# Attention's output product, sum and norm by token halves, and a later entry of the second half into the gated expert network

## The reference

```python
x = x + L2_xattn(layernorm(x), ctx, ctx, Wq, bq, Wk, bk, Wv, bv, Wo, bo)
x = x + L2_ffn(layernorm(x), router_w, w_gate, w_up, w_down)

def _pruned_attention(q, k, v):            # 16 heads of width 8, per batch
    scores = softmax(q @ k.T / sqrt(8))
    keep = int(S * 0.9)
    col_sum = scores.sum(axis=queries)
    mask = top_k(col_sum, keep)            # keys kept, per head
    return (scores * mask) @ v             # then @ Wo.T + bo

def _L2_ffn_ref(x, router_w, w_gate, w_up, w_down):   # 8 experts, top 2
    cw = normalised top-2 weights of softmax(x @ router_w.T)
    for e in experts:
        acc += cw[:, e] * ((silu(x @ wg[e]) * (x @ wu[e])) @ wd[e])
```

## Time and profile before

| what | value |
|---|---|
| median of 3 runs | 847.29 us (846.08 to 850.32) |
| profiled execution, its own time | 840.29 us |
| its span, first to last instruction | 838.6 us |
| mean granted TensorE clock | 0.920 of full |
| pruned attention's last steps, hand-over and step 0 of ffn2 | about 594 to 625 us of the span |
| plain attention's end | about 71 to 79 us of the span |

### The profile page before, as it was taken

How to read it: one execution, slowest core, us unless ns; L and a number is a source line. 1 busy time by engine, 2 the same in 40 slices (tenths; PEclk the granted TensorE clock), 3 DMA queues, 4 the chain that set the end, 5 groups by cost and what they waited for, 6 DMA issues and landing times. The chain is left out here.

```text
span 838.6 us, 14511 instructions
## 1 busy us (share of the span) xinstructions
PE 725.6 (87%) x4910; PEld 605.2 (72%) x4910; DVE 558.4 (67%) x1478; ACT 416.3 (50%) x1279; POOL 373.8 (45%) x375
## 2 busy tenths in 40 slices
PE   6884799998899999988579999699769999994755
PEld 3553699997899998876467887466558888883754
DVE  6897664355899998874746776668555565655535
ACT  3991344344455555552245776489334466651221
POOL 6753312202566643533214775664331588872001
PEclk9898799999999999997879999779779999996678
DMA  7000011110000000000004443000101322100000
GB/s 271 2 1 26 14 42 36 50 50 1 1 1 2 7 2 1 2 1 0 20 23 150 128 137 132 1 2 2 39 26 36 106 87 89 62 2 1 1 0 25
DMA packets 14276, 33.11 MB, mean 39 GB/s; under 512 B 1744, under 2 KB 5864, under 8 KB 13952
## 3 DMA queue, kind: packets, MB, share of 16 engines
q1 hardware_dynamic: 14208, 32.26, 11.6%
HBM read 31.63 MB, written 0.62 MB: 38 GB/s over the span
## 5 line engine op out<-in xcount | busy, mean ns | idle before, releaser
L1210 PE MATMUL banks<-input_hi,weights_in_lo 128*128 128x512 f32 x296 | 125.2, 423 | 17.8 <-PEq L1571 9.7
L1210 PE MATMUL banks<-input_lo,weights_in_hi 128*128 128x512 f32 x296 | 120.1, 406 | 0.0
L1210 PE MATMUL banks<-input_hi,weights_in_hi 128*128 128x512 f32 x296 | 119.7, 404 | 0.0
L1210 PEld LDWEIGHTS banks<-weights_out,hidden 128*128 128x128 f32 x864 | 100.5, 192 | 8.1 <-issue 5.1
L1210 PE MATMUL banks<-weights_out,hidden 128*128 128x128 f32 x864 | 101.6, 276 | 5.2 <-PEq L1524 4.5
L987 ACT ACTIVATE probabilities<-banks,neg_max 128x128 f32<-128x128 f32 x256 | 90.7, 430 | 13.2 <-DVE neg_max L1896 13.2
L1076 ACT ACTIVATE hidden<-banks,cols 128x512 f32<-128x512 f32 x80 | 54.1, 688 | 77.6 <-ACTq L1074 77.6
L697 POOL TENSOR_TENSOR rstd<-var_eps,neg_half 128x4 f32<-128x4 f32 x24 | 24.8, 1034 | 145.4 <-POOLq L696 130.3
L1210 PEld LDWEIGHTS banks<-input_hi,weights_in_lo 128*128 128x128 f32 x296 | 58.5, 198 | 31.9 <-issue 19.1
L807 POOL TENSOR_TENSOR hidden<-hidden,scratch 128x512 f32<-128x512 f32 x48 | 62.0, 1292 | 19.3 <-ACT hidden L1095 16.6
L1210 PEld LDWEIGHTS banks<-input_hi,weights_in_hi 128*128 128x128 f32 x296 | 58.2, 197 | 13.2
(11 more groups left out here) (272 smaller groups left out, 1754.4 us busy)
## 6 DMA issues: line engine op xcount, KB each, us to landing
scratch<-cw_rows SPq DMA_DIRECT2D x19, 512.0 KB, 4.0
weights_out<-w_in SPq DMA_DIRECT2D x17, 256.0 KB, 2.7
weights_in<-w_in SPq DMA_DIRECT2D x8, 512.0 KB, 3.6
weights_in<-w_in SPq DMA_DIRECT2D x9, 256.0 KB, 3.1
weights_in<-w_in SPq DMA_DIRECT2D x16, 128.0 KB, 2.2
weights_out<-w_in SPq DMA_DIRECT2D x16, 128.0 KB, 2.1
wq<-w1q_in SPq DMA_DIRECT2D x1, 1024.0 KB, 4.8
wo<-w1o_in SPq DMA_DIRECT2D x1, 1024.0 KB, 6.9
```

The lines of the kernel that those rows point to most:

```text
L1210: return pe.matmul(o, l, rh, start=start, stop=stop, **kw)
```

## The change

1. `attention_output` takes a half and a bank on TensorE and VectorE. In the plain attention both halves are still done at the end, in banks 4 and 5, but half 0 waits only for its own four blocks of `attT`.
2. In the pruned attention half 0's product is a stage of TensorE's list, `first_output`, in step 17, behind the last column sums, into bank 0. Its sum, statistics and norm are a stage of VectorE's list in step 19, behind the last `keep_values` and ahead of the last `scale_kept` (step 20).
3. After the attention TensorE turns half 0 of `xn` first and then makes half 1's product, into bank 7. VectorE runs `split_input(0)`, then half 1's sum, statistics and norm.
4. `second_half_at` is `(1, 0)` for every network: ffn2's second half is turned, taken and split at the head of step 1.

GpSimd's and SyncE's code is unchanged.

```diff
             def second_half_at(self):
-                return (0, 2) if self.FC == 4 and self.E > 1 else (1, 0)
+                return (1, 0)
...
+            def attention_output(prune, weight, half, at):            # TensorE
+                pe.wait_ge(out_copied[prune], (2 if prune else 4) * (half + 1))
+                for i in range(4):
+                    b = 4 * half + i
+                    m = mm(b4(at)[:, i, :], attT[:, b * P:(b + 1) * P], weight)
+                m.then_inc(y_attn_done, 1)
...
+                def first_output(it, n):
+                    pe.wait_ge(exps_done[prune], 8 * 15)
+                    attention_output(prune, w("wo2"), 0, 0)
...
-                                   (column_sums, range(UNITS), 2), (values_kept, last, 5)],
+                                   (column_sums, range(UNITS), 2), (first_output, (0,), 17),
+                                   (values_kept, last, 5)],
...
-            def attention_output(prune, weight):
-                pe.wait_ge(out_copied[prune], 4 if prune else 8)
-                for b in range(NB):
-                    m = mm(b4(4 + b // 4)[:, b % 4, :], attT[:, b * P:(b + 1) * P], weight)
-                    if b % 4 == 3:
-                        m.then_inc(y_attn_done, 1)
...
-                    if s == 0:
-                        transpose_half(0, source, f.output_bank(0))
-                    if s == 1 and f.FC == 2:
-                        transpose_half(1, source, f.output_bank(1))
+                    if s == 0 and not f.gated:
+                        transpose_half(0, source, f.entry_bank(0))
+                    if s == 1:
+                        transpose_half(1, source, f.entry_bank(1))
...
-                        if s == 0 and f.FC == 4 and fc == 2:
-                            transpose_half(1, source, f.output_bank(1))
...
-            attention_output(False, w("wo0"))
+            attention_output(False, w("wo0"), 0, 4)
+            attention_output(False, w("wo0"), 1, 5)
...
             narrow_attention(True)
-            attention_output(True, w("wo2"))
+            transpose_half(0, xn, ffn2.entry_bank(0))
+            attention_output(True, w("wo2"), 1, 7)
             mixed(ffn2, None, xn, w("r2"))
...
+            def attention_output(half, at):                           # VectorE
+                if half == 0:
+                    dve.wait_ge(x_bias_ready, 1)
+                    dve.sem_inc(x_bias_ready, -1)
+                dve.wait_ge(y_attn_done, 1)
+                dve.sem_inc(y_attn_done, -1)
+                part = x[:, 4 * half:4 * half + 4, :]
+                dve.tensor_tensor(part, part, b4(at), ALU.add).then_inc(st.sem, st.one())
+                norm_stats(half, x, 1e-5)
...
+                def first_output(it, n):
+                    attention_output(0, 0)
+                    norm_apply(0, x, xn, norm_tok_ready)
...
-                                    (keep_values, last, 4), (scale_kept, last, 5), (rank_first, last, 2),
+                                    (keep_values, last, 4), (first_output, (0,), 19), (scale_kept, last, 5),
+                                    (rank_first, last, 2),
...
-                            if (s, fc) == (0, 2):
+                            if (s, fc) == f.second_half_at():
                                 split_input(1)
...
             narrow_attention(True)
-            attention_output()
-            for half in range(2):
-                norm_apply(half, x, xn, norm_tok_ready)
             split_input(0)
+            attention_output(1, 7)
+            norm_apply(1, x, xn, norm_tok_ready)
             mixed(ffn2, [])
```

More of the change, by code:

```diff
@@ L1494, in hidden @@
                     for fc in range(f.FC):
-                        if source is not None and first and (n, fc) == (0, 2) == f.second_half_at():
-                            transpose_half(1, source, f.entry_bank(1))
                         if f.FC == 4 and begun and not f.gated:
@@ L1990, in narrow_attention @@
                                     (copy_both, range(UNITS), 2)], UNITS, 1, st.close)
-            def attention_output():
-                dve.wait_ge(x_bias_ready, 1)
-                dve.sem_inc(x_bias_ready, -1)
-                for half in range(2):
[L1997 to L2001, removed]
             def mlp_norm(half, *args):
@@ L2337, in _ @@
             narrow_attention(False)
-            attention_output()
+            attention_output(0, 4)
+            attention_output(1, 5)
             for half in range(2):
```

## The result

The changed kernel takes 835.83 us (median of 4 executions, 833.65 to 838.15) where the kernel before takes 848.68 (4 executions): ratio 0.9852, 95% interval 0.9809 to 0.9894. The profiled execution took 833.65 us, 6.6 less than that of before, close to the forecast of 834.3. The two numbers don't agree: 6.6 by the profiles, 12.9 by the medians. Later executions settle it in between. The 81 executions of before that were timed beside the experiments have a mean of 844.4 us (standard error 0.3), and 17 of the changed kernel one of 835.8 (0.6): 8.6 us.

What follows compares the result with a forecast made beforehand. One chain passing between engines from keep_values to the gated network bounds the hand-over. Step 1 earlier 5.77, plain attention 0.74, clock -0.5: 6.0 us saved, 847.29 to 841.3 us, range 837.5 to 845.5.

Steps and rivals of the forecast that it cites:

- the early passes before 598: TensorE ahead of the mask: half 0's eight product passes fit into 2.51 us of idle time, priced at nothing.
- a new pause before step 1: Gated network: four turned blocks, then TensorE idle 2.2 to 2.5 us before step 1, a sign of being right.
- signs of being wrong: TensorE waiting for half 1's product or norm, gates holding half 1's split, clock 0.50 over much of step 1, late GpSimd power.
- The plain attention: End of the plain attention: half 0's product need not wait for the last block's scaling, 0.74 us saved.
- The later entry: Half 1 turned at step 1's head: gives back 2.4 of 8.2 us, so step 1 begins 5.77 earlier.
- the rest shifts as a block: Behind step 1 of the gated network: all that follows is shifted by whatever step 1 is shifted.
- The clock, both ends: TensorE's clock: 0.85 us gained entering step 0, 1.35 lost in the pause before step 1; together 0.5 against the change.
- Rival 2: Clock is up at step 0's entry and stays: 8.2 us saved, 839.1 us; chance 0.10.
- The 1.35 for the new pause: Before step 1: half of the 2.7 us that a clock fallen in TensorE's pause would cost at worst.
- the way to step 0: From keep_values through half 0's sum, norm, turning and split: first network matmul at 608.61 against 616.79, 8.18 us earlier.
- The two waits ahead of the add: VectorE ahead of half 0's add: two waits with semaphore decrements, 0.26 us each.
- The rule on shared ports: VectorE beside GpSimd at half 1's norm: priced by the row at 1.48 us; by the rule the sum would be 6.16, not 6.51.

Runs made afterwards that it cites:

- The run with the pauses of before filled: Kernel before with idle products in TensorE's pauses, six ahead of turning half 0 and two behind it: 843.0 us, ratio to before 0.9980.
- the filled run: Changed kernel with ten idle 128x512 matmuls in TensorE's pause before step 1, behind the turning of half 1: 833.8 us, ratio to before 0.9877.
- the variants: Six edits of the changed kernel: half 1 entering before chunk 2 or 3, idle matmuls before step 1, GpSimd's split held, and two combinations: ratios to before 0.9869 to 0.9927.
- the run with GpSimd held: Changed kernel with GpSimd's split of the second expert's weights held until ScalarE has done step 1's first chunk: ratio to before 0.9906.

## Why the prediction was off

**Right.** Faster, and for the reasons given, in the order given: the early passes before 598, the power on GpSimd at 602.44 for "near 602.5", `scale_kept` late and hidden, half 1's product ended (606.98) before step 0 began, a new pause before step 1. Two of the signs of being wrong appeared in part: step 1 ran at 0.50 for 3.1 of its 7.1 us, and VectorE's split of half 1 came right behind the gates. The gates cost nothing, since GpSimd's subtraction ended only at 616.22. The plain attention gives 0.80 for 0.74. The later entry gives back, as an own run shows. That the rest shifts as a block holds to 0.5 us (202.1 on average in five traces, 202.6 in four, so 0.5 longer); among all traces it runs from 200.3 to 203.7.

**Luck.** The forecast for the profiled execution, 834.3, came within 0.7 of the measured one by chance: the hand-over shortened by 7.4 and not by 5.3, and stretches that the change does not touch happened to be about 1.6 longer in that pair.

**The step that failed is "The clock, both ends".** It put 0.85 for the entry, half of what a step 0 at full clock would gain, and took the cold stretch of before, 8.00 us for 24 matmuls, as the base. Step 0 took 5.57 (607.80 to 613.37), 2.43 less. It was not an even chance: in all ten traces with half 0 made early the granted clock was 0.99 or 1.00 from step 0 to step 1, and in the five of before it was 0.66 to 0.73. The run with the pauses of before filled shows that idle time ahead of step 0 sets it. Rival 2 had the entry right and was given 0.10. The 1.35 for the new pause, half of 2.7, was near: 1.56 (against the filled run) to 1.65 (against before) measured, in four of four traces of the changed kernel.

The terms add up for the first pair of traces, from `keep_values` to step 2: forecast 5.77 + 0.85 - 1.35 = 5.27; step 0's clock 1.58 more than priced (2.43 less 0.85), the way to step 0 1.30 more, the later entry 0.46 less, the pause's clock 0.29 less. That makes 7.40, as measured (37.84 less 30.44).

**The same oversight at the other end of the path.** I counted TensorE's work ahead of the norm at the duration that the trace of before showed. It has two: 3.64 or 3.06 for the 64 small matmuls, 3.78 or 2.05 for the 16 passes. Before, the small matmuls and the first eight passes are on the path, and the way from `keep_values` to step 0 is 16.9 or 18.4. Afterwards VectorE's early norm lies beside them and only the turning of half 0 is left: 8.95, or 9.4 in the variants. So of 1.5 us that the clock could cost there 0.5 is left. The sum had no term for it.

**Sizes.** The way to step 0 was forecast as 10.24 from the start of `keep_values` (608.61 less 598.37) and took 8.94. The two waits ahead of the add cost nothing, 0.5 less than priced; variance to norm took 1.43 for 1.63; turning, taking and splitting half 0 took 2.86 for 3.33, since turning ran at full clock. Against that, step 1 came 3.54 behind the start of turning half 1 instead of 3.08.

**The rule on shared ports.** The prediction went by the row, 1.48 for half 1's norm and nothing more for the split. They took 1.72 and 1.14, and the run with GpSimd held shows that 0.71 us of delay come from this. In all seven traces of the changed kernel and its variants in which GpSimd was not held, VectorE's split of half 1 ended 0.54 to 0.56 behind the end of GpSimd's subtraction (616.22, then 616.77), whether it took 1.14 or 1.69. The Trainium skill, page "SBUF — State Buffer", section "Who interferes with whom", says that a VectorE instruction with two inputs in SBUF contends with a GpSimd one that reads SBUF, and with this the traces agree. For the norm, a `tensor_scalar`, no trace shows a wait until GpSimd's instruction ends: of four instructions one took 0.945 for 0.338, and all four were done by 612.90, when GpSimd's, begun at 611.00 for 2.78, was not over. The prediction named both sides of the rule. It rejected the one on `tensor_scalar` for the norm, and never asked about the other for the split, though that is VectorE's last instruction before step 1.

**The base.** 841.3 was 6.0 below a median of three executions that lay 2.9 above the mean of 81. With that mean the forecast would have been 838.4 and the measured 835.8, and a range as wide would have taken it in: that the time fell outside is in part the bad luck of three long executions in the base. The gain of 8.6 us (standard error 0.7) against the forecast 6.0 remains, and so does the step that failed.

**What the traces account for.** From `keep_values` to step 2, 37.0 on average in five traces of before and 30.45 in four of the changed kernel: 6.6. The plain attention 0.8. Together 7.4, the rest shifted by 0.5 the other way. 8.6 less 7.4 is 1.2, less than two standard errors, and up to 1.7 with the 0.5. In the stretch from the first network to `keep_values`, which the edits hardly touch, traces differ from 507.7 to 517.3 us. Whether a part of the 1.2 is real stays open.

## What to carry to other kernels

Where the engine that multiplies idles ahead of a dense stage, closing the pause is worth the pause and the slow matmuls behind it, so price both, and price a new pause in the same way. Moving another engine's work next to slow products takes their clock off the path. Before crediting an edit with a change of the clock, see whether its trace already differed ahead of the edit; here six variants did. For each instruction that ends a wait, ask what GpSimd reads at that time. And where executions of one kernel differ by 10 us and more, compare stretches of several traces, not two whole executions: 7.4 of 8.6 us are found so, and an effect of 0.80 at one place is read from the trace while the time can't show it.

## What was not expected of the hardware

One stretch of one kernel, at the same instructions, has few lengths and not a spread: 35.7 to 35.8 or 37.8 to 37.9 us before, and 30.43 to 30.46 in four traces after. A pause of 2.24 us (2.83 from the start of turning) let the granted clock fall when the later entry was made alone (0.86 from step 1 to step 2), and did not when GpSimd was held (1.00). The two traces differ already in the small matmuls ahead of step 0: 3.01 in the first, 3.64 in the second. Of the six traces with an unfilled pause of 2.2 to 3.0 before step 1 the clock fell in the five in which they took 3.0 to 3.1, and held in the one in which they took 3.64. One trace is too few to call that a rule. Idle products ahead of step 0 brought the clock to 1.00 in the kernel before; that they also kept it up in the changed kernel's pause is not shown.
